# Reordering the outset of a decoder layer's projection phase on four engines' queues

## The reference, cut to what matters

```
q = silu(dwconv(hs @ Wq, conv_q))          # 4 taps, per channel
k = silu(dwconv(hs @ Wk, conv_k))
v = silu(dwconv(hs @ Wv, conv_v))
beta = sigmoid(hs @ Wb)
q, k = l2norm(q), l2norm(k)                # x * rsqrt(sum(x*x) + 1e-6)
attn = where(strict, -(k*beta @ k^T), 0)   # per chunk of 32 tokens
T = inv(eye - attn)
paths = dwconv(v, fir_s), dwconv(v, fir_m), dwconv(v, fir_l), delta rule, v
```

## Time and profile before

| what | value |
|---|---|
| median of 3 runs | 971.71 us (969.2 to 977.56) |
| profiled execution | 980.14 us, its span 978.3 us |
| mean granted TensorE clock of the span | 0.952 |
| busy: PE, PEld, DVE, ACT, POOL | 89%, 67%, 62%, 46%, 35% |
| chain that ended last: PE, DVE, ACT, POOL, issue, DMA | 60%, 14%, 10%, 7%, 4%, 3% |

### The profile page before, as it was taken

One profiled execution on the slowest core, in us unless ns is written; L12 is line 12 of the kernel. 1 busy time (PEld: TensorE's weight loads), 2 busy tenths in 40 slices (PEclk: granted clock), 3 DMA queues, 4 the chain that ended last, 5 costly groups with the idle time before them and its releaser, 6 DMA issues.

```text
span 978.3 us, 18379 instructions
## 1 busy us (share of the span) xinstructions
PE 870.4 (89%) x6875; PEld 654.3 (67%) x6875; DVE 605.2 (62%) x1410; ACT 453.0 (46%) x845; POOL 345.7 (35%) x336
## 2 busy tenths in 40 slices
PE   7799789789999987998889888979997999999994
PEld 5577566667777765786556555656785777777774
DVE  5799797566889888432557777774462343333255
ACT  5788656446677766342144544445331322222221
POOL 9422200123557566312001343223540242222684
PEclk9999999778999997998799999999999999999998
DMA  5699769897455432124991222002302222221421
GB/s 168 202 269 281 203 153 250 296 240 172 109 119 120 76 76 78 32 86 165 388 338 42 63 63 88 12 24 80 100 23 83 66 60 60 66 66 50 151 65 64
DMA packets 144468, 123.52 MB, mean 126 GB/s; under 512 B 89790, under 2 KB 126590, under 8 KB 143102
## 3 DMA queue, kind: packets, MB, share of 16 engines
q1 hardware_dynamic: 140974, 112.98, 41.0%
q0 software_dynamic: 3408, 9.38, 2.6%
HBM read 74.04 MB, written 48.29 MB: 125 GB/s over the span
## 4 chain that ended last, share of the span: by engine, by line
PE 60%; DVE 14%; ACT 10%; POOL 7%; issue 4%; DMA 3%; SPq 1%; POOLq 0%; DVEq 0%; ACTq 0%; another core or an unknown queue 0%
PE ps L2513 10%; PE ps L1919 6%; PE ps L2528 5%; DVE cross_room L1952 4%; PE ps L1859 3%; PE ps L2377 3%; PE ps L1352 3%; PE ps L666 3%; PE ps L1620 3%; POOL hank L345 2%; PE ps L1981 2%; POOL kept L2660 2%; PE ps L2390 2%; PE ps L423 2%; DMA hank<-rt_dram 2%
## 5 line engine op out<-in xcount | busy, mean ns | idle before, releaser
L1997 ACT ACTIVATE cross_room<-ps 128x1024 f32<-128x1024 f32 x64 | 65.5, 1023 | 99.1 <-PE ps L1923 96.9
L1952 DVE TENSOR_REDUCE cross_room<-ps 128x4 f32<-128x1024 f32 x64 | 78.1, 1224 | 39.3 <-PE ps L1919 38.5
L2513 PE MATMUL ps<-wr,xbT 128*128 x312 | 99.0, 459 | 1.8 <-ACT xbT L2549 1.8
L1919 PE MATMUL ps<-kept,cross_room 32*128 32x256 f32 x512 | 74.1, 411 | 21.7 <-DVE cross_room L1952 18.8
L2602 POOL DMA_INDIRECT y_dram<-yb,dest_row x39 | 37.5, 961 | 134.6 <-DVE dest_row L2578 130.4
L1320 POOL TENSOR_TENSOR st<-st,exponent 128x20 f32<-128x20 f32 x16 | 56.9, 3554 | 64.7 <-DVE st L1295 63.4
L2513 PEld LDWEIGHTS ps<-wr,xbT 128*128 128x128 f32 x312 | 58.8, 189 | 29.5 <-issue 2.5
L1923 PE MATMUL ps<-cross_room,kept 32*128 32x256 f32 x512 | 75.3, 413 | 0.0
L1919 PEld LDWEIGHTS ps<-kept,cross_room 32*128 32x128 f32 x512 | 47.1, 190 | 39.7 <-issue 21.7
L550 DVE SCALAR_TENSOR_TENSOR room<-room 128x256 f32<-128x256 f32 x144 | 58.4, 480 | 11.4 <-ACT room L499 11.4
L2587 DVE TENSOR_TENSOR cross_room<-cross_room,ps 128x352 f32<-128x352 f32 x39 | 20.3, 521 | 58.6 <-PE ps L2513 57.1
(11 more groups left out here) (353 smaller groups left out, 2243.2 us busy)
## 6 DMA issues: line engine op xcount, KB each, us to landing
xs_dram<-params SPq DMA_DIRECT2D x17, 1040.0 KB, 17.9
room<-in_gW SPq DMA_DIRECT2D x8, 1280.0 KB, 7.7
tok_dram<-room SPq DMA_DIRECT2D x8, 768.0 KB, 6.4
fir_dram<-room SPq DMA_DIRECT2D x6, 1024.0 KB, 7.3
paths<-fir_dram SPq DMA_DIRECT2D x48, 128.0 KB, 3.7
xb<-xs_dram SPq DMA_DIRECT2D x39, 130.0 KB, 2.3
hank<-rt_dram SPq DMA_DIRECT2D x8, 512.0 KB, 8.1
yr<-y_dram SPq DMA_DIRECT2D x16, 256.0 KB, 3.2
```

The costliest lines, as they stand in the source:

```text
L1919: m1 = nc.tensor.matmul(ps[:, c, t * T:(t + 1) * T], strips(qS[b % 3], g, c)[:, t * P:(t + 1) * P], kS(b, g)[c * CH:(c + 1) * CH], start=T ...
L1952: V.tensor_reduce(mx[:, :, g, XD + 2 * h * CH:XD + (2 * h + 1) * CH + 1:CH].rearrange("p t c -> p c t"), ps[:, pair(h), :].rearrange("p c ...
L1997: S.activation(pT[g % 2][:, pair(h)].rearrange("p c k t -> p (c k t)"), ps[:, pair(h), :].rearrange("p c n -> p (c n)"), ACT.Exp).then_inc ...
L2513: m = nc.tensor.matmul(ps[:, 2 * (j % 2) + half, 0:FF], xbT[j % 2][:, k, :], wr[:, bass.ds(e, 1), k, half, :].rearrange("p e n -> p (e n)" ...
```

## The change

Seven edits, all in the first phase:

1. POOL clears `hank[0..2]` at once (nine instructions); `hank[3]` (three) and `win` (one) are cleared between its first and second normalise stage.
2. SP's `sp_filters` is no longer ahead of round 2 but beside it, so that the fetch of batch 2's tokens and gate rows stands in front of the nine filter stores.
3. `s.weights` becomes five semaphores: one each for Wq, Wk, Wv and Wb, and one for the three tap arrays. PE waits for each matrix right before it uses it; ACT and DVE wait for the taps alone.
4. PE makes eight transposes of the identity into bank 7 of PSUM as soon as the identity is there; nothing reads them.
5. PE makes three more of these after it has turned batch 0's tokens.
6. ACT's first instruction is a Silu of one column of 128 partitions, into a place of `beta` that is written again later.
7. The list of signals given back after the phase has the new names.

```diff
--- before.py
+++ after.py
@@ -243,7 +243,7 @@
 def phase_project_invert_and_fir(pg, a, env):
     nc, pe, act, dve, pool, sp = pg.nc, pg.pe, pg.act, pg.dve, pg.pool, pg.sp
     V, S, G = nc.vector, nc.scalar, nc.gpsimd
-    s = pg.signals("Project", "weights wpad_zero wpad raw_zero sel_zero sel_made filters_turned filters_copied filters_out xT_turned xT_copied raw_made raw_copied beta_made tanh beta first mac silu "
+    s = pg.signals("Project", "wq_in wk_in wv_in wb_in taps_in wpad_zero wpad raw_zero sel_zero sel_made filters_turned filters_copied filters_out xT_turned xT_copied raw_made raw_copied beta_made tanh beta first mac silu "
                    "sums_made sums_copied small_zero conv_turned sq v_copied ss rn_step tok kT_turned kT_copied a_made diag win_zero win_made fir_made stage_copied small_in tau_log eps_exp small",
                    "x_in rows_in sums_out tok_out diag_out am_in inv_set inv_step turned inv_out")
     with ExitStack() as mem:
@@ -298,15 +298,27 @@
                 r = n * ROW % CH
                 V.memset(sel[i][0:DH, n, r:r + 1], lo).then_inc(*s.sel_made.up())
                 V.memset(sel[i][DH:P, n, r + 1:r + 2], hi).then_inc(*s.sel_made.up())
+        W_IN = (s.wq_in, s.wk_in, s.wv_in)
+
+        def pe_idle_turns(n):
+            for _ in range(n):
+                nc.tensor.transpose(ps[:, 7, 0:P], ident[:], ident[:])
+
+        def act_first_table():
+            S.activation(env.beta[:, 0, 0:1], env.exponent[:, 0, 0:1], ACT.Silu)
+
+        pe.wait_ge(env.constant, 2)
+        pe_idle_turns(8)
         for e in (pe, act, dve):
             e.wait_ge(env.constant, env.constant.made)
+        act_first_table()
         act.wait_ge(s.raw_zero, 1)
 
         def sp_weights():
-            for w, src in zip((*W, wb), (a["Wq"], a["Wk"], a["Wv"], a["Wb"])):
-                nc.sync.dma_start(w[:], src.rearrange("(k p) n -> p k n", p=P)).then_inc(*s.weights.up(16))
+            for w, src, landed in zip((*W, wb), (a["Wq"], a["Wk"], a["Wv"], a["Wb"]), (*W_IN, s.wb_in)):
+                nc.sync.dma_start(w[:], src.rearrange("(k p) n -> p k n", p=P)).then_inc(*landed.up(16))
             for j, src in enumerate((a["conv_q"], a["conv_k"], a["conv_v"])):
-                nc.sync.dma_start(taps[:, j], src.rearrange("(k p) i -> p k i", p=P)).then_inc(*s.weights.up(16))
+                nc.sync.dma_start(taps[:, j], src.rearrange("(k p) i -> p k i", p=P)).then_inc(*s.taps_in.up(16))
             sp.wait_ge(s.wpad_zero, 1)
             for f, n_taps in enumerate(FIRS):
                 nc.sync.dma_start(wpad[:, :, f, P - n_taps:P],
@@ -337,9 +349,10 @@
                                       filters[:, k, r]).then_inc(*s.filters_out.up(16))
             sp.wait_ge(env.hank_zero, 1)
             nc.sync.dma_start(env.rt_dram[:, :, P:P + BLK].rearrange("s f n c -> n (s f) c"), no_taps).then_inc(*s.filters_out.up(16))
-
-        def pool_hank_zero():
-            for h in env.hank:
+            yield
+
+        def pool_hank_zero(*slices):
+            for h in (env.hank[sl] for sl in slices):
                 for f in range(NF):
                     pool.in_turn()
                     G.memset(h[:, f].rearrange("k s c -> k (s c)"), 0.0).then_inc(*pool.tick(env.hank_zero))
@@ -409,10 +422,11 @@
             i = b % 2
             if b == 0:
                 pe_turn_x(0)
-            yield
-            pe.wait_ge(s.weights, s.weights.made)
+                pe_idle_turns(3)
+            yield
             pe.wait_ge(s.xT_copied, b + 1)
             for j in range(3):
+                pe.wait_ge(W_IN[j], 16)
                 pe.wait_ge(s.raw_copied, 3 * (b - 1) + j + 1)
                 if j == 0:
                     pe.wait_ge(s.sums_copied, b)
@@ -424,6 +438,7 @@
                                              start=(k == 0), stop=(k == KT - 1))
                 m.then_inc(*s.raw_made.up())
                 yield
+            pe.wait_ge(s.wb_in, 16)
             for t in range(TT):
                 for k in range(KT):
                     m = nc.tensor.matmul(ps[:, 0, t * H:(t + 1) * H], xT[:, k, t * P:(t + 1) * P], wb[:, k, :], start=(k == 0),
@@ -488,7 +503,7 @@
             if b == 0:
                 act_copy_x(0)
             yield
-            act.wait_ge(s.weights, s.weights.made)
+            act.wait_ge(s.taps_in, 16 * 3)
             for j in range(3):
                 act.wait_ge(s.raw_made, 3 * b + j + 1)
                 act.wait_ge(s.mac, 18 * (b - 1) + 6 * (j + 1))
@@ -537,7 +552,7 @@
         def dve_project(b):
             i = b % 2
             yield
-            dve.wait_ge(s.weights, s.weights.made)
+            dve.wait_ge(s.taps_in, 16 * 3)
             for j in range(3):
                 dve.wait_ge(s.raw_copied, 3 * b + j + 1)
                 for tap in range(1, TAPS):
@@ -749,7 +764,7 @@
             G.memset(win[HS[0]].rearrange("p c (b n) w -> p (c b) n w", n=NBLK)[:, :, 0, :], 0.0).then_inc(*pool.tick(s.win_zero))
 
         last = B + 1
-        weave([sp_fetch, sp_project, sp_normalise], B, {2: sp_filters}, {4 + sl: sp_first_hank(sl) for sl in range(RING)})
+        weave([sp_fetch, sp_project, sp_normalise], B, {}, {2: sp_filters()} | {4 + sl: sp_first_hank(sl) for sl in range(RING)})
         sp_triangles(B - 1)
         weave([idle, pe_project, pe_normalise], B, {2: pe_filters}, {last: pe_fir()})
         weave([idle, act_project, act_normalise], B, {2: act_filters})
@@ -757,9 +772,8 @@
         weave([idle, dve_project, dve_normalise], B, beside={last: dve_invert(0)})
         env.second = dve_invert(1)
         interleave([in_rounds(env.second, range(12))])
-        pool_win_zero()
-        pool_hank_zero()
-        weave([idle, idle, pool_normalise], B)
+        pool_hank_zero(0, 1, 2)
+        weave([idle, idle, pool_normalise], B, {3: lambda: (pool_hank_zero(3), pool_win_zero())})
         pool_small_zero()
     env.sp_stage = sp_stage
     env.sp_inverses, env.sp_late_hank, env.sp_small, env.dve_small, env.projected = sp_inverses, sp_late_hank, sp_small, dve_small, s
@@ -2707,7 +2721,7 @@
         env.top = lambda n, shape, dt=F32: ctx.enter_context(nc.sbuf_tensor(n, shape, dt, side="right"))
         env.xs_dram = nc.dram_tensor("xs_dram", [NE * STRIDE + P, XW], F32).ap()
         place_cross_parameters(env)
-        env.done = ("wpad_zero", "wpad", "sel_zero", "sel_made", "filters_turned", "filters_copied", "xT_turned", "xT_copied",
+        env.done = ("wq_in", "wk_in", "wv_in", "wb_in", "taps_in", "wpad_zero", "wpad", "sel_zero", "sel_made", "filters_turned", "filters_copied", "xT_turned", "xT_copied",
                     "beta_made", "tanh", "first", "mac", "silu")
         pg.leave([x for name, x in env.projected._asdict().items() if name in env.done])
         place_tokens_kept(nc, env)
```

## The result

Over 20 runs of each the changed kernel took 970.18 us (median) and the kernel before 974.38. The ratio is 0.9937, 95% interval 0.9909 to 0.9965: 0.6% or 6.1 us less (3.4 to 8.9). Each ratio leaves out the executions that ran in a slower state (here 4 of the 20 of the changed kernel and 2 of the other 20), which is why it gives 6.1 us where the two medians are 4.2 apart. A second timing, beside the first experiments, gave 0.9898 (0.9847 to 0.9949), from three executions of the changed kernel. The profiled execution's span is 969.7 us, 8.6 less than before.

The account below looks back on a forecast made before the run. POOL's clearing ahead of the norms, leaving DVE idle, was taken to bound the first 62 us. Outset 3.1 + clearing 3.11 + clock 1.24 = 7.45 us, from 971.71 to 964.3 us; range 956 to 973.

Parts of the forecast that it names:

- The clearing: POOL, first rounds: nine pieces instead of twelve and win ahead of the first norms end DVE's idle time, saving 3.11 us.
- The clock after PE's gap: PE after its gap from 29.4 to 33.4 us: slow-clock work goes, saving 1.24 us, bounds 0 and 1.24.
- The outset: Pipeline start: earlier projections, idle turns and a closed 0.28 us gap save 3.1 us together, bounds 1.8 and 3.8.
- the early bound: PE's first matmuls: clock rises at 5.3 us, all projections fast; 3.8 us for the outset, giving 963.6.
- My 7.2 us: PE's first matmuls: assumed time of the clock's rise, 1.6 + 5.6, losing 0.7 us at half speed.
- The table load: ACT's start: load runs from about 3.1 to 4.4 while ACT waits; tokens' copy at 5.08 instead of 6.38.
- The tokens ahead of the stores: SP, batch 2: fetch out by about 20 us, cost 0; behind the filter stores it would take back 1 to 3 us.
- The rival with the clearing in DVE's way: DVE's tap instructions of batches 1 and 2: held for all 7.4 us of moved clearing, giving 971.7; chance 0.04.
- What the first two rounds win is carried along: Rounds after the first two: no engine is tied to a fixed time, so their gain lasts.
- The later clock: Delta rule: an earlier outset shifts PE's gaps; clock falls may change by one, giving 972.9 or 955.7; chances 0.14 and 0.16.
- one fall more or fewer: Delta rule: one clock fall of some 20 us costs or saves 8.6 us; chances 0.14 more, 0.16 fewer.
- The rival with half the outset: Outset: turns don't lift the clock, 1.8 us saved instead of 3.1, 1 us lost to fetch or store; 966.8; chance 0.14.

Follow-up runs that it names:

- e9: Changed kernel with each batch's tokens fetched one round earlier, at the head of SP's round; ratio 0.9900 to the kernel before, span 963.6 us.
- e3: Changed kernel with POOL's clearing in the order of before (win, all twelve pieces, then the norms); ratio 1.0000 to the kernel before, span 977.4 us.
- first execution: First of two profiled executions of the same kernel; for the changed kernel, span 969.7 us, for the kernel before 978.3 us.
- e4: Changed kernel with the filters' stores ahead of batch 2's tokens again; ratio 0.9886 to the kernel before, span 967.3 us.
- e8: Changed kernel with SP's read-back of the triangles a round later, behind the next fetch of tokens; ratio 0.9945 to the kernel before, span 974.4 us.
- e2: Changed kernel profiled a second time and timed, no edit; ratio 0.9898 to the kernel before, span 968.7 us.
- e12: Changed kernel with each tap buffer cleared by one memset instead of three; span 969.4 us, timed once, no ratio.
- e1: Kernel before, profiled a second time, no edit; span 977.3 us, no ratio.
- first pair: First profiled executions of the kernel before and of the changed kernel, no further edit; spans 978.3 and 969.7 us.
- e6: Changed kernel without the eleven idle transposes on PE; ratio 0.9944 to the kernel before, span 956.1 us.
- e7: Changed kernel with beta's multiply-add made by ACT instead of DVE; ratio 0.9877 to the kernel before, span 968.4 us.
- e10: Changed kernel with tokens fetched a round sooner and beta's multiply-add on ACT together; ratio 0.9918 to the kernel before, span 963.9 us.

## Why the prediction was right, point by point

The direction and the size were right: 6.1 us (3.4 to 8.9) measured, 7.45 forecast. The absolute figure, 964.3 against 970.18, is off by 5.9 us, 2.7 of it because the forecast started from a median of three executions (971.71) and that of twenty is 974.38. That the first two spans differ by 8.6 us, near the forecast, is luck: 3.7 of it are not the change. By its steps:

*The clearing.* Right. L574 came without idle time; from batch 1's first copy to L574 it is 26.93 - 20.95 = 5.98 us instead of 32.08 - 22.90 = 9.18, so 3.20 where 3.11 was forecast. POOL was free in time for both norms; the second started at 34.68, 0.09 us behind the sum. In the executions with the quickest outset POOL was late for the first norms, in e9 at 20.77 for a sum that was there at 20.09, and DVE's multiplication still had no idle time ahead of it, as forecast for a small delay. e3 shows that the gain of the first phase hangs on this edit, and its ratio of 1.0000 says the same of the whole.

*The clock after PE's gap.* Right: the granted clock is 1.00 from 30 to 40 us in both executions, and from L574 to the next first copy it is 33.55 - 26.93 = 6.62 us in the second (6.63 forecast). In the first it was 7.18, of which 0.66 is the held beta line; so only 0.69 of the 1.24 us were gained there. A slip without effect: 0.93 of the window from 37 us puts the rise before the change at 37.14 us, not 37.07.

*The outset.* Right within its bounds (1.8 to 3.8). DVE's tap instructions of batch 0 ended at 20.07 before, at 17.30 in the first execution (2.77 sooner) and at about 18.1 in the second (2.0). Batch 1's first copy won only 1.95 us, as the held beta line stands between the two in the first execution, and batch 2's fell at 34.11 and 33.55 where about 32.5 was given as the sign. The rise of the clock was the unknown, and it varies from execution to execution of the same kernel: 6.61 and 7.69 us for the same 24 matmuls. Six other kernels with the turns took 5.46 to 5.55 us, which is full speed throughout, the early bound. The Trainium skill, page "TensorE: Matmul & The Clock Gate" (What's actually happening), says that activity releases the throttle and that the point of the transition varies with where the first matmul falls. The rows agree that it varies, and by more than the half microsecond either way that the page gives: the estimates of the rise run from before 5.7 to 10.2 us, with the first turns at 1.59 or 1.60 each time. My 7.2 us lay within that spread; that it came near the first execution's 7.9 is luck.

*The table load.* The copy of the tokens came at 4.94 instead of 6.38, 5.08 forecast. The load's place was not as told: it ran at 0.80, ahead of ACT's wait for the constants, not at 3.1. Forecast and result agree in this, but no run tests edit 6 alone.

*The tokens ahead of the stores.* Right: e4 lost 2.03 us of PE to that wait (1 to 3 forecast), and 16.12 - 13.09 = 3.0 us from batch 1 to 2 beside e8, whose outset was as quick.

*The rival with the clearing in DVE's way.* I gave it 4 in 100 and priced it at all of 7.4 us. The part that I checked was right: the tap instructions, with two SBUF inputs, take 7.21/18 = 401 ns beside the clearing. The part that I didn't look for was in the trace before: L556 at 0.64 us beside a memset and 0.17 without. The page "Advanced Engine Details and Errata" of the Trainium skill (Mode Summary) ties the interference to DVE's two-port modes; e2 and e12 show the interference for this one instruction, a tensor_scalar from SBUF to SBUF; which mode it ran in, no run shows. It cost 1.44 us in the first execution and nothing in the second.

*"What the first two rounds win is carried along."* It held in the pair e1 and e2 (7.54 us at batch 2, 8.6 at the end) and failed in the first pair (5.84 at batch 2, 2.16 at batch 7). I reasoned that no engine is tied to a fixed time and gave the transfers of the later rounds no thought. From 50 to 102 us of the first execution the DMA engines' busy share is 0.99 to 1.13 in every window of four microseconds, and batch 7 came 16.91 - 12.74 = 4.2 us late, in the second 4.5. The interval from batch 6 to 7 was 14.03 and 16.66 us before and 16.91 and 17.25 after, but 12.74 in e6 and e7. So the wait is older than the change and varies by execution. Full queues alone don't make it, since e6 has shares of 1.00 to 1.09 in the same windows. Whether starting earlier makes it longer on average stays open. e8 speaks against SP's order as its cause, and in e9 and e10, with a round of lead, there was none.

*The later clock.* The rivals priced one fall more or fewer at 8.6 us; their own product, 20 x 5.5/13.04, gives 8.4, which moves no bound by more than 0.2. (The rival with half the outset names 1 us lost, but its 966.8 neither adds that nor takes off the 1.24; with both it is 966.6.) The size was about right. e6's span is 956.1 us, 12.6 below the second execution of the changed kernel. 3.0 of it are there at the FIR matmuls, and 9.8 more come between these and the cross attention, which starts at 436.6 instead of 449.4 us. The granted clock differs most from 200 to 240 us, 1.00 in e6 (first row) and 0.73 in e2 (second):

```profile
200.00:240.00 40.00, 36.35 (x486) 1.00 0.87 180
```

```profile
200.00:240.00 40.00, 37.83 (x372) 0.73 0.86 204
```

That the clock is the whole reason is not shown. Over the executions of the changed kernel and its variants the stretch from the FIR matmuls to the cross attention took 323.8 to 338.1 us, a spread larger than the gain.

## What to carry to other kernels

Ask of each filler job (a memset, a store) which small result behind it in the same queue is awaited, and put the job into the engine's next gap; the trace shows the waiting engine's idle time, 3.11 us here, before anything is built. When the DMA engines are busy throughout the rounds that follow, a transfer on the path can eat part of what an earlier start won, in one execution and not in the next. Another place in SP's order didn't help here (e8); a round of lead was followed by no wait in two executions (e9, e10), which is a hint and no proof. Profile at least two executions of each kernel before a difference of single microseconds is put down to an edit, and compare them at landmarks along the way, not only at the end.

## What was not expected of the hardware

- A DVE tensor_scalar of 128x8 from SBUF to SBUF ended with the GpSimd memset that ran when it began, in all 20 cases (after 0.37 to 2.85 us instead of 0.17), while scalar_tensor_tensor went on (401 ns each beside the clearing, 410 with POOL idle), and so did a copy from PSUM when no held line stood ahead of it (0.68 us in e7). The copy behind the held line ended with it, so holds under 0.7 us were free.
- The same kernel's first 24 matmuls took 6.61 and 7.69 us in two executions (started at 5.58 and 5.71), while the profile's granted clock read 1.00 in both.
- The issue of one DMA on SP, 0.4 us otherwise, took up to 6.09 us while the DMA engines were busy throughout, whichever transfer it was.
